# A perceiver layer with a mixture of experts: first loads in slices, last value tiles stored singly, middle stage and experts in one block, a value product ahead of local scores

## The chip, the cores and the metric

The kernel runs on one core of one Trainium2 chip, as one program. The metric is the time of one execution on the device, in microseconds (us). Three runs of the kernel before are given with their median, and beside them one profiled execution. TensorE is called PE, its weight loads PEld, VectorE DVE, ScalarE ACT, GpSimd POOL, and SP is the engine that issues most DMAs.

## The reference, cut to what matters

```python
x = x + xattn(layernorm(x), ctx, ctx, mask)     # 16 heads, 2 x 512 queries, 2 x 8192 keys
x = x + attn(layernorm(x))                      # local: window of 7 keys, latent 32x32 map on keys and values
x = x + ffn(layernorm(x))                       # shared MLP + 16 experts
def ffn(x):                                     # h = x as 1024 tokens of 512
    scores = sigmoid(h @ gate_w.T)
    topk_score, topk_ids = top_k(scores.T, 128) # each expert takes its 128 best tokens
    xin = h[topk_ids]
    eo = silu(xin @ gw.T + gb) * (xin @ up_w.T + up_b)      # 512 -> 2048
    eo = eo @ down_w.T + down_b                             # 2048 -> 512
    out = zeros.at[topk_ids].add(eo * topk_score)
    return out + (silu(x @ sh_gate.T) * (x @ sh_up.T)) @ sh_down.T
```

Everything is float32. Where the kernel multiplies in the fast format fp32r it splits both operands into a high and a low part and adds three products (high by high, high by low, low by high).

## The kernel before

The engines run programs of their own, written out by hand, and meet at semaphores. The program is cut into blocks; at the end of a block all five engines wait for one another.

**Context stage** (block at L176). The context (32 tiles of 512 tokens) is read tile by tile into CX; ACT makes the high part CH, DVE the low part CL, and PE makes keys (`keys`, L421: four banks, each 12 matmuls over the four quarters c of the contraction index) and values (`values`, L429). ACT and DVE evict, SP stores keys and values to memory (`stores`, L209 to L216). Ahead of the loop SP loads the key weights WK, the first context tile, the tokens X and then small constants (L218 on); ACT and DVE split WK and the tile, PE makes the first keys; DVE normalises X (`emit_layernorm`, L109 to L123), PE turns the normal tiles (L449) and makes the queries (L459). The last context tile is stored by `stores(NC_ALL - 1, 1)`: two key stores, then, when all four value tiles (128 tokens each, L286) are evicted, four value stores, one for each group of heads.

**Between** lies a block (L500) that is skipped unless a bound on the scores fails. The flag is read by every engine.

**Attention** (block at L666). Scores (L721), exponentials (L796, L799), value products (L734), sums on DVE (L832). PE starts it with seven scores of data loaded during the context stage.

**Middle stage** (block at L933). Output projection, local attention, shared MLP, routing. PSUM banks 0 to 3 are used in turn in the order of the list ORDER: `claim` waits until the bank's earlier result is evicted, `filled` and `evicted` are the waits for a result and for its eviction. Local attention runs in `slot(b, k)` steps: PE turns the weights of step k - 2 (L1062) and makes the scores of step k + 1 (L1051, into banks 4 and 5), which must wait until DVE has scaled the scores of step k out of those banks (L1463); DVE then takes the maximum (L1468), ACT the exponentials (L1300), DVE normalises (L1487, L1490) and copies the turned weights out (L1481). Products of the middle stage (`product`, L1028) stand between slots: q0.. queries, k1.. keys, v0.. values, vl0.. latent values (L1039). The end of the stage: down products dn4 to dn7 (L1117), each added to X by DVE (L1507) and stored by SP (L998); between them the routing result is turned, DVE makes the token numbers, and POOL gathers the first expert's rows (L1010). PE turns those rows (`rows0`, L1262) after dn7. DVE splits the bias tables and the first three weight tiles (`weights_lo`, L883) between its additions.

**Experts** (block at L1622). 192 weight tiles of 1 MB pass through a ring of six raw buffers (SP, L871), ACT makes the high part (L878), DVE the low part (L883), and PE makes gate and up products (L1663, bias L1652), turns the hidden rows (L1683) and makes the down products (L1699). POOL gathers the other experts' rows (L1631) and scatters the results (L1645).

## Time and profile before

| | us |
|---|---|
| median of 3 runs | 2913.43 (2911.68 to 2914.97) |
| profiled execution | 2915.47 |
| its span, first to last instruction | 2913.7 |
| PE busy | 2856.8 (98%) |
| DVE busy | 2153.7 (74%) |
| ACT busy | 1697.8 (58%) |
| POOL busy | 90.0 (3%) |

A line of 40 digits gives the busy tenths of each engine in 40 equal slices of some 73 us; 9 is 90% or more. PEclk is the granted clock of PE in tenths of full speed.

```profile
PE   7999999999899999999999999999999999999998
PEld 4888888888644444344444443445554588888887
DVE  5544444444498989898989898957466798888887
ACT  3112111211398989898989898925351377777775
PEclk9999999999999999999999999999999999999999
```

The chain of waits, followed back from the last instruction, by engine and by line:

```profile
PE 20%; POOL 0%; DVE 0%; issue 0%; ACT 0%
PE PS L1663 12%; PE PS L1699 6%; PE PS L1652 1%; PE PS L1683 1%; PE PS L1712 0%; POOL out L1645 0%; DVE YO L1790 0%; DVE HTL L1778 0%; ACT HTH L1740 0%
```

Slices 1 to 11 are the context stage, 12 to 26 attention, 27 to 32 the middle stage, the rest the experts.

### The profile page before, as it was taken

To read this page: it belongs to the slowest core of one execution; us is meant where nothing else is said; L and a number is where in the kernel's file an instruction comes from. 1 tells how busy PE (TensorE), PEld (TensorE's weight loads), DVE (VectorE), ACT (ScalarE), POOL (GpSimd) and SP (SyncE) were. 2 spreads that over 40 slices of the span, in tenths; PEclk is the share of its full clock that TensorE was granted. 3 is DMA by queue.
4 is the path that set the end of the run, shared out by engine and by line. 5 is a ranking of instruction groups with operands and counts; after the bars stand their busy time and mean duration, and the time that the engine had idled before them with its cause. 6 is when DMAs were issued, how large, how long until landed. Compare 5 with 4: busy or idle time off the path is not lost. (4 is left out here: it accounts for less than half of the span.)

```text
span 2913.7 us, 36671 instructions
## 1 busy us (share of the span) xinstructions
PE 2856.8 (98%) x14229; PEld 1752.3 (60%) x14229; DVE 2153.7 (74%) x1586; ACT 1697.8 (58%) x2128; POOL 90.0 (3%) x43
## 2 busy tenths in 40 slices
PE   7999999999899999999999999999999999999998
PEld 4888888888644444344444443445554588888887
DVE  5544444444498989898989898957466798888887
ACT  3112111211398989898989898925351377777775
POOL 0000000000000000000000000000000320000000
PEclk9999999999999999999999999999999999999999
DMA  5555555555555555555555555520103399999995
GB/s 207 181 186 188 192 182 187 188 193 182 171 131 128 128 124 125 127 132 124 128 122 131 128 128 125 124 71 24 64 13 129 143 391 345 346 346 349 347 348 201
DMA packets 228186, 515.46 MB, mean 177 GB/s; under 512 B 17986, under 2 KB 83906, under 8 KB 198460
## 3 DMA queue, kind: packets, MB, share of 16 engines
q1 hardware_dynamic: 224460, 505.15, 55.1%
q0 software_dynamic: 3584, 8.39, 1.2%
q8 instruction: 92, 1.51, 0.2%
q14 instruction: 50, 0.41, 0.0%
HBM read 400.03 MB, written 113.44 MB: 176 GB/s over the span
## 5 line engine op out<-in xcount | busy, mean ns | idle before, releaser
L832 DVE TENSOR_TENSOR AC<-AC,PR 128x2048 f32<-128x2048 f32 x440 | 969.6, 2281 | 0.0
L796 ACT ACTIVATE PR<-PS 128x1024 f32<-128x1024 f32 x866 | 831.7, 1034 | 78.9 <-PE PS L721 78.8
L721 PE MATMUL PS<-QS,KS 128*128 128x512 f32 x2048 | 607.9, 422 | 22.2 <-PEq L500 8.8
L721 PEld LDWEIGHTS PS<-QS,KS 128*128 128x128 f32 x2048 | 345.4, 188 | 388.3 <-ACT PR L796 260.1
L734 PE MATMUL PS<-PR,VC 128*32 128x512 f32 x4096 | 492.5, 598 | 1.1 <-ACT PR L796 1.1
L883 DVE TENSOR_TENSOR WL<-RAW,WH 128x2048 fp32r<-128x2048 f32 x192 | 436.2, 2286 | 60.8 <-ACT WH L878 60.8
L370 ACT ACTIVATE KH<-PS,bk_s 128x512 fp32r<-128x512 f32 x128 | 88.0, 688 | 561.0 <-PE PS L421 561.0
L878 ACT ACTIVATE WH<-RAW 128x2048 fp32r<-128x2048 f32 x192 | 361.8, 1913 | 1.3 <-PEq L933 1.1
L277 DVE SCALAR_TENSOR_TENSOR KL<-PS,bk_s,KH 128x512 fp32r<-128x512 f32 x128 | 95.7, 750 | 268.7 <-ACT KH L370 268.7
L734 PEld LDWEIGHTS PS<-PR,VC 128*32 128x32 f32 x4096 | 106.9, 109 | 247.0 <-issue 245.6
L421 PE MATMUL PS<-CH,WKH 128*128 128x512 f32 x512 | 203.2, 397 | 12.5 <-DVE CL L272 12.5
L421 PE MATMUL PS<-CL,WKH 128*128 128x512 f32 x512 | 203.3, 397 | 0.0
L429 PE MATMUL PS<-WVH,CH 128*128 128x512 f32 x512 | 203.1, 397 | 0.0
L421 PE MATMUL PS<-CH,WKL 128*128 128x512 f32 x512 | 203.0, 397 | 0.0
L429 PE MATMUL PS<-WVH,CL 128*128 128x512 f32 x512 | 202.6, 396 | 0.0
L429 PE MATMUL PS<-WVL,CH 128*128 128x512 f32 x512 | 202.5, 396 | 0.0
L1663 PE MATMUL PS<-WL,XEH 128*128 128x512 f32 x512 | 201.1, 393 | 0.0
L1663 PE MATMUL PS<-WH,XEL 128*128 128x512 f32 x512 | 200.6, 392 | 0.0
L1663 PE MATMUL PS<-WH,XEH 128*128 128x512 f32 x512 | 200.4, 391 | 0.0
L286 DVE TENSOR_TENSOR VS<-PS,bv_s 128x512 f32<-128x512 f32 x128 | 85.1, 685 | 113.0 <-PE PS L429 113.0
L799 ACT ACTIVATE PR<-PS 128x512 f32<-128x512 f32 x158 | 95.6, 605 | 58.5 <-PE PS L721 58.5
L1740 ACT ACTIVATE HTH<-PS 128x512 fp32r<-128x512 f32 x64 | 38.3, 599 | 150.7 <-PE PS L1683 150.7
(200 smaller groups left out, 3298.3 us busy)
## 6 DMA issues: line engine op xcount, KB each, us to landing
KS<-kh_d SPq DMA_DIRECT2D x256, 256.0 KB
RAW<-in_gw SPq DMA_DIRECT2D x64, 1024.0 KB, 5.6
RAW<-in_up_w SPq DMA_DIRECT2D x64, 1024.0 KB, 5.1
RAW<-in_down_w SPq DMA_DIRECT2D x64, 1024.0 KB, 5.1
AT<-in_ctx SPq DMA_DIRECT2D x32, 1024.0 KB, 5.7
kh_d<-KH SPq DMA_DIRECT2D x32, 1024.0 KB, 4.4
kl_d<-KL SPq DMA_DIRECT2D x32, 1024.0 KB, 6.5
v_d<-VS SPq DMA_DIRECT2D x128, 256.0 KB, 3.0
```

Of the source, the lines that this page charges most:

```text
L277: v.scalar_tensor_tensor(KL[s][:, g, :], PS[:, g, :], bk_s[:, g:g + 1], KH[s][:, g, :].bitcast(F32), ALU.add, ALU.subtract).then_inc(s_kl, 1)
L370: nc.scalar.activation(KH[s][:, g, :], PS[:, g, :], ACT.Identity, bias=bk_s[:, g:g + 1]).then_inc(s_kh, 1)
L421: mm = pe.matmul(PS[:, g, :], w[:, c, g * P:(g + 1) * P], a[s][:, c, :], start=(k == 0), stop=(k == len(terms) - 1))
L429: mm = pe.matmul(PS[:, G + t, :], a[s][:, c, t * P:(t + 1) * P], w[:, c, :], start=(k == 0), stop=(k == len(terms) - 1))
L721: mm = pe.matmul(PS[:, take(*BANK[m]), :], KS[N % 2][:, j, t * P:(t + 1) * P], QS[bg % 2][:, j, :], start=True, stop=True)
L734: m = pe.matmul(PS[j * DH:(j + 1) * DH, OUTB, :], VC[N % 2][:, t, j * DH:(j + 1) * DH], PR[tile % BUFS][:, j, :], start=q == 0, stop=q == ...
L796: nc.scalar.activation(PR[tile % BUFS][:, 2 * hp:2 * hp + 2], PS[:, first:first + 2, :], ACT.Exp, scale=SCALE).then_inc(s_exp, 1)
L799: nc.scalar.activation(PR[tile % BUFS][:, 2 * hp], PS[:, first, :], ACT.Exp, scale=SCALE)
L832: v.tensor_tensor(a[i % 2][:], a[i % 2][:], p[:], ALU.add).then_inc(s_acc, 1)
L878: nc.scalar.activation(WH[n % PAIRS][:], RAW[:, n % RAWS], ACT.Copy).then_inc(s_hi, 1)
L883: nc.vector.tensor_tensor(WL3[n % PAIRS][:], RAW[:, n % RAWS], WH[n % PAIRS][:].bitcast(F32), ALU.subtract).then_inc(s_lo, 1)
L1663: m = pe.matmul(PS[:, bank, :], x[e % 2][:, c, :], w[:, c, :], start=False, stop=i == len(terms) - 1)
```

## The change

- The first loads go by quarters of the contraction index: SP issues WK quarter 0, context quarter 0, WK quarter 1 and so on, eight loads of 256 KB, then X in four loads of two token tiles. ACT and DVE split each quarter as it comes. PE makes the first keys with the quarter as the outer loop and the four banks within. The layernorm statistics wait for their pair of tiles.
- The last context tile's values are stored tile by tile: each of the four stores holds 128 tokens of all groups and waits for its own eviction.
- The experts' programs stand in functions called at the end of the middle stage's block; the end of block between them is gone. In its place PE waits for the evictions of dn5, dn6 and dn7 ahead of the first expert product. `rows0` is made ahead of dn7, with its place in ORDER changed; DVE splits the rows' low part ahead of adding dn7. ACT splits the fifth weight tile only when dn7 is complete. POOL's further gathers start when the bias tables are ready; SP's seventh weight tile follows the store of dn7.
- In local attention v00 goes ahead of scores 0, v01 ahead of slot 0, v02 between slots 1 and 2, v03 between slots 2 and 3.

```diff
             v = nc.vector
             for i in range(TT):
+                if i % 2 == 0:
+                    chain.engine.wait_ge(s_x[i // 2], 16)
                 n = chain.mark(v.bn_stats(tmp[:, i, 0:6], src[:, i, :]))
...
-                sp.dma_start(WK[:].bitcast(F32), wk).then_inc(s_wk, 16)
-                sp.dma_start(CX[0], ctx_t[0]).then_inc(s_cx[0], 16)
-                sp.dma_start(X[:], x.rearrange("(i p) d -> p i d", p=P)).then_inc(s_x, 16)
+                for c in range(DC):
+                    sp.dma_start(WK[:, c].bitcast(F32), wk[:, c]).then_inc(s_wk[c], 16)
+                    sp.dma_start(CX[0][:, c], ctx_t[0][:, c]).then_inc(s_c0[c], 16)
+                for i in range(TT // 2):
+                    sp.dma_start(X[:, 2 * i:2 * i + 2], x[2 * i * P:(2 * i + 2) * P].rearrange("(i p) d -> p i d", p=P)).then_inc(s_x[i], 16)
...
-                stores(NC_ALL - 1, 1)
+                n, s = NC_ALL - 1, 1
+                sp.wait_ge(s_kh, n * G + G)
+                sp.dma_start(kh_d[:, n].rearrange("g p k -> p g k"), KH[s][:].bitcast(F32)).then_inc(s_kvst[s], 16)
+                sp.wait_ge(s_kl, n * G + 2 * G)
+                sp.dma_start(kl_d[:, n].rearrange("g p k -> p g k"), KL[s][:].bitcast(F32)).then_inc(s_kvst[s], 16)
+                for t in range(KT):
+                    sp.wait_ge(s_vs, n * KT + KT + t + 1)
+                    sp.dma_start(v_d[:, n, :, t, :].rearrange("g p d -> p g d"),
+                                 VS[s][:, t, :].rearrange("p (g d) -> p g d", g=G)).then_inc(s_kvst[s], 16)
...
-                dve.wait_ge(s_whi, 1)
-                v.tensor_tensor(WKL[:], WK[:].bitcast(F32), WKH[:].bitcast(F32), ALU.subtract).then_inc(s_wlo, 1)
-                split(0, 0)
-                dve.wait_ge(s_x, 16)
+                for c in range(DC):
+                    last = c == DC - 1
+                    if last:
+                        dve.wait_ge(s_whi, 1)
+                    else:
+                        dve.wait_ge(s_fhi, 2 * c + 1)
+                    v.tensor_tensor(WKL[:, c], WK[:, c].bitcast(F32), WKH[:, c].bitcast(F32), ALU.subtract
+                                    ).then_inc(s_wlo if last else s_flo, 1)
+                    if last:
+                        dve.wait_ge(s_chi, 1)
+                    else:
+                        dve.wait_ge(s_fhi, 2 * c + 2)
+                    v.tensor_tensor(CL[0][:, c], CX[0][:, c], CH[0][:, c].bitcast(F32), ALU.subtract
+                                    ).then_inc(s_clo if last else s_flo, 1)
                 emit_layernorm(chain, X, XN, tmp, s_xn, 1)
                 dve.wait_ge(s_small, 80)
                 key_lows(0, 0)
...
-                act.wait_ge(s_wk, 16)
-                nc.scalar.activation(WKH[:], WK[:].bitcast(F32), ACT.Copy).then_inc(s_whi, 1)
-                split(0, 0, 0)
+                for c in range(DC):
+                    last = c == DC - 1
+                    act.wait_ge(s_wk[c], 16)
+                    nc.scalar.activation(WKH[:, c], WK[:, c].bitcast(F32), ACT.Copy).then_inc(s_whi if last else s_fhi, 1)
+                    act.wait_ge(s_c0[c], 16)
+                    nc.scalar.activation(CH[0][:, c], CX[0][:, c], ACT.Copy).then_inc(s_chi if last else s_fhi, 1)
...
-                pe.wait_ge(s_wlo, 1)
-                keys(0, 0)
+                for c in range(DC):
+                    if c < DC - 1:
+                        pe.wait_ge(s_flo, 2 * c + 2)
+                    else:
+                        pe.wait_ge(s_wlo, 1)
+                        pe.wait_ge(s_clo, 3)
+                    for g in range(G):
+                        for k, (w, a) in enumerate(((WKH, CH), (WKH, CL), (WKL, CH))):
+                            mm = pe.matmul(PS[:, g, :], w[:, c, g * P:(g + 1) * P], a[0][:, c, :],
+                                           start=(c == 0 and k == 0), stop=(c == DC - 1 and k == 2))
+                        if c == DC - 1:
+                            mm.then_inc(s_kps, 1)
...
-                 + [f"{w}1{f}" for f in range(FS) for w in "gu"] + ["dn4", "dn5", "topk", "dn6", "dn7", "rows0"])
+                 + [f"{w}1{f}" for f in range(FS) for w in "gu"] + ["dn4", "dn5", "topk", "dn6", "rows0", "dn7"])
...
+        def experts_gpsimd(pool):
+            def gather(e, landed):
+                nc.gpsimd.indirect_dma_start(XG[e], None, h_d, bass.IndirectOffsetOnAxis(ap=token[:, e:e + 1], axis=0)
+                                             ).then_inc(landed, 16)
+
+            pool.wait_ge(s_bs, 5)
+            gather(1, s_g1)
+            for e in range(2, 7):
+                gather(e, s_ga)
+            pool.wait_ge(s_out, 16 * TT)
+            for e in range(7, E):
+                gather(e, s_gb)
+            for e in range(E):
...
+            def gate(S):
+                if S >= 2:
+                    pe.wait_ge(s_si, S - 1)
+                if S == 0:
+                    evicted(pe, "rows0")
+                elif S % FC == 0:
+                    pe.wait_ge(s_xl, S // FC)
+                rows_product("g", S, S % 2)
...
+            pe.wait_ge(s_bs, 5)
+            for name in ("dn5", "dn6", "dn7"):
+                evicted(pe, name)
+            gate(0)
+            up(0)
...
+            for n in range(EARLY, 4):
+                split(n)
+            filled(act, "dn7")
+            for n in range(4, PAIRS):
+                split(n)
+            silu(0)
...
+                pe.wait_ge(s_wv6, 16)
+                product("v00", WV6, XT2[0], 0)
                 pe.wait_ge(s_ke, G)
                 evicted(pe, "q03")
                 scores(0, 0)
-                pe.wait_ge(s_wv6, 16)
+                product("v01", WV6, XT2[0], 1)
                 slot(0, 0)
-                product("v00", WV6, XT2[0], 0)
                 slot(0, 1)
-                product("v01", WV6, XT2[0], 1)
+                product("v02", WV6, XT2[0], 2)
                 slot(0, 2)
-                product("v02", WV6, XT2[0], 2)
+                product("v03", WV6, XT2[0], 3)
                 slot(0, 3)
-                product("v03", WV6, XT2[0], 3)
                 slot(0, 4)
                 for i in range(4, TT):
                     evicted(pe, f"t2{i}")
...
                 down(6)
-                down(7)
                 pe.wait_ge(s_g0, 16)
                 bank = claim(pe, "rows0")
                 for c in range(DC):
                     m = pe.transpose(PS[:, bank, c * P:(c + 1) * P], XG0[:, c * P:(c + 1) * P], ident[:])
                 m.then_inc(s_full[bank], 1)
+                down(7)
+                experts_tensor(pe)
...
                     weights_lo(dve, i - 5)
+                    if i == TT - 1:
+                        bank = filled(dve, "rows0")
+                        dve.wait_ge(s_xh, 1)
+                        v.tensor_tensor(XEL[0][:], PS[:, bank, :].rearrange("p (c t) -> p c t", c=DC), XEH[0][:].bitcast(F32),
+                                        ALU.subtract).then_inc(s_free[bank], 1)
                     add_down(i)
-                bank = filled(dve, "rows0")
-                dve.wait_ge(s_xh, 1)
-                v.tensor_tensor(XEL[0][:], PS[:, bank, :].rearrange("p (c t) -> p c t", c=DC), XEH[0][:].bitcast(F32),
-                                ALU.subtract).then_inc(s_xl, 1)
...
-                pool.wait_ge(s_to, 2)
-                gather(1, s_g1)
```

## Rows read from the trace of the kernel before

**Rows 1.** Table of stages: stretch, length, busy us (instructions) per engine, granted clock, DMA share, GB/s.

```profile
2330.00:2890.00 560.00, 560.00 (x2611) 462.68 (x2610) 498.91 (x332) 401.88 (x319) 59.32 (x19) 1.00 0.95 348
```

**Rows 2.** Timeline, start: start us, duration, engine, line, operation, shapes, [idle before <- releaser].

```profile
2.12 2.39 SPq L221 DMA_DIRECT2D ident<-in_ident  x1
...
5.67 1.91 ACT L374 ACTIVATE WKH<-KL 128x2048 fp32r<-128x2048 f32 x1 [3.65 <-DMA KL<-in_wk]
...
8.16 1.91 ACT L366 ACTIVATE CH<-AT 128x2048 fp32r<-128x2048 f32 x1 [0.58 <-DMA AT<-in_ctx]
...
10.11 2.29 DVE L272 TENSOR_TENSOR CL<-AT,CH 128x2048 fp32r<-128x2048 f32 x1 [0.20 <-ACT CH L366]
...
12.50 0.77 PE L421 MATMUL PS<-CH,WKH 128*128 128x512 f32 x1 [12.50 <-DVE CL L272]
...
17.33 0.47 PE L421 MATMUL PS<-CH,WKL 128*128 128x512 f32 x1
```

**Rows 3.** Timeline, start, layernorm statistics, normal tiles, and PE's next work.

```profile
14.11 4.85 DVE L109 BATCH_NORM_STATS2 ln_tmp<-X 128x6 f32<-128x512 f32 x8 [1.71 <-DMA X<-in_x]
...
21.21 3.75 DVE L123 TENSOR_SCALAR XN<-X,ln_tmp 128x512 f32<-128x512 f32 x8
...
26.03 1.04 PE L449 MATMUL PS<-ident,XN 128*128 128x128 f32 x8
```

**Rows 4.** DMA issues of the first 60 us: count, KB each, median us to landing.

```profile
qh_d<-QH SPq DMA_DIRECT2D x6, 256.0 KB, 2.1
```

**Rows 5.** Timeline of DVE, SP and PE, context stage to attention.

```profile
773.53 0.69 DVE L286 TENSOR_TENSOR VS<-PS,bv_s 128x512 f32<-128x512 f32 x1 [1.86 <-PE PS L429]
...
774.25 2.64 SPq L216 DMA_DIRECT2D v_d<-VS  x4
...
782.21 3.32 PE L721 MATMUL PS<-QS,KS 128*128 128x512 f32 x7 [8.78 <-PEq L500]
```

**Rows 6.** Timeline of PE and DVE, first local scores.

```profile
1975.56 1.14 PE L1051 MATMUL PS<-RAW,AT 32*122 32x128 f32 x16 [0.87 <-ACT AT L1274]
...
1978.18 1.14 PE L1051 MATMUL PS<-RAW,AT 32*122 32x128 f32 x16 [1.49 <-DVE EX L1463]
...
1979.25 5.40 PE L1028 MATMUL PS<-XT,WV 128*128 128x512 f32 x8
...
2002.25 3.70 PE L1028 MATMUL PS<-XT,WK 128*128 128x512 f32 x8
...
2013.61 1.05 PE L1071 MATMUL PS<-EX,RAW 128*32 128x122 f32 x32 [1.09 <-DVE RAW L1455]
...
2003.95 1.22 DVE L1463 SCALAR_TENSOR_TENSOR EX<-PS,RAW 122x1024 f32<-122x1024 f32 x1
```

**Rows 7.** Groups by line: shapes, count | busy us, mean ns | idle before, releasers.

```profile
L1463 DVE SCALAR_TENSOR_TENSOR EX<-PS,RAW 122x1024 f32<-122x1024 f32 x20 | 24.4, 1218 | 17.9 <-PE PS L1051 17.8
...
L1300 ACT ACTIVATE EX<-EX,NX 122x128 f32<-122x128 f32 x160 | 61.9, 389 | 16.0 <-PE PS L1062 11.7 <-DVE NX L1468 4.0
```

**Rows 8.** Table of stages, columns as in group 1, two stretches of low clock.

```profile
1980.15:1983.50 3.35, 3.35 (x5) 1.35 (x4) 2.51 (x4) 2.42 (x14) 0.00 (x0) 0.50 0.00 0
...
2307.83:2311.20 3.37, 3.37 (x9) 2.61 (x10) 1.73 (x1) 3.37 (x2) 2.44 (x3) 0.50 0.77 275
```

**Rows 9.** Timeline of PE, DVE and POOL, middle stage to experts.

```profile
2292.08 2.72 POOL L1010 DMA_INDIRECT AT<-h_d,token  x1 [101.18 <-DVEq L1599]
...
2298.66 0.68 DVE L1507 TENSOR_TENSOR X<-X,PS 128x512 f32<-128x512 f32 x1
...
2305.20 0.60 PE L1262 MATMUL PS<-ident,AT 128*128 128x128 f32 x4
...
2305.40 0.69 DVE L1507 TENSOR_TENSOR X<-X,PS 128x512 f32<-128x512 f32 x1 [1.06 <-PE PS L1117]
...
2307.70 0.64 PE L1652 MATMUL PS<-BIAS,PICK 128*128 128x512 f32 x1 [1.90 <-PEq L933]
...
2309.47 4.49 DVE L883 TENSOR_TENSOR WL<-RAW,WH 128x2048 fp32r<-128x2048 f32 x2 [2.24 <-ACT WH L878]
```

More of the change, by code:

```diff
@@ L931, in program @@
         YO = [se(f"YO{i}", [CAP, D]) for i in range(2)]
+        s_g1, s_ga, s_gb = sem("second_gathered"), sem("tokens_gathered"), sem("last_tokens_gathered")
+        s_si, s_hid, s_t, s_hth, s_htl, s_xt, s_y, s_sc = (sem(n) for n in (
+            "expert_silu", "expert_hidden", "hidden_turned", "hidden_hi", "hidden_lo",
+            "expert_rows_turned", "expert_output", "expert_scattered"))
+        XG = [XG0] + [AT[:, i, :] for i in range(2, 8)] + [X[:, i, :] for i in range(TT)] + [WO[:, 3, :]]
@@ new lines, in experts_sync @@
+        def experts_sync(sp):
+            for n in range(RAWS, len(TILES)):
+                load_raw(sp, n)
+        def experts_gpsimd(pool):
[10 more added lines that the diff above has]
+            for e in range(E):
+                pool.wait_ge(s_y, e + 1)
+                if e:
+                    pool.wait_ge(s_sc, 16 * e)
+                nc.gpsimd.indirect_dma_start(out, bass.IndirectOffsetOnAxis(ap=token[:, e:e + 1], axis=0), YO[e % 2][:], None,
+                                             compute_op=ALU.add).then_inc(s_sc, 16)
+            pool.wait_ge(s_sc, 16 * E)
@@ new lines, in experts_scalar, with silu, hidden_hi, rows_hi @@
+        def experts_scalar(act):
+            def silu(S):
+                act.wait_ge(s_used, NTH["g", S] + 1)
+                if S >= 2:
+                    act.wait_ge(s_hid, S - 1)
+                nc.scalar.activation(GE[S % 2][:], PS[:, S % 2, :], ACT.Silu).then_inc(s_si, 1)
+            def hidden_hi(S):
+                act.wait_ge(s_t, S + 1)
+                if S >= 2:
+                    act.wait_ge(s_used, NTH["d", S - 2] + 1)
+                nc.scalar.activation(HTH[S % 2][:], PS[:, 4, :].rearrange("p (f t) -> p f t", f=FT), ACT.Copy).then_inc(s_hth, 1)
+            def rows_hi(e):
+                act.wait_ge(s_xt, e)
+                if e >= 2:
+                    act.wait_ge(s_used, NTH["u", (e - 1) * FC - 1] + 1)
+                nc.scalar.activation(XEH[e % 2][:], PS[:, 7, :].rearrange("p (c t) -> p c t", c=DC), ACT.Copy).then_inc(s_xh, 1)
+            def split(n):
+                if EARLY <= n < len(TILES):
+                    weights_hi(act, n)
+            for n in range(EARLY, 4):
[4 more added lines that the diff above has]
+            silu(0)
+            for S in range(STEPS):
+                if S % FC == 2 and S // FC + 1 < E:
+                    rows_hi(S // FC + 1)
+                split(3 * S + PAIRS)
+                hidden_hi(S)
+                split(3 * S + PAIRS + 1)
+                if S + 1 < STEPS:
+                    silu(S + 1)
+                split(3 * S + PAIRS + 2)
@@ L1011, in _ @@
                                              ).then_inc(s_g0, 16)
+                experts_gpsimd(pool)
             @block.tensor
```

279 lines of the change are left out of this document (107 added, 172 removed).

## The prediction

> **What bounds the kernel now.** I read the page's totals and its 40 slices first: TensorE (PE) is busy in nine tenths or more of nearly every slice, so only those places matter where PE stands still or runs at half clock. The chain of waits that ended last lies on PE all the way back to the first expert product, and the table of stages shows why: in 560 us of the expert stage PE is busy for 560.00 while VectorE (DVE) has 61 us to spare [rows 1]. What comes ahead of such a stage moves its end one for one. So I went through the timeline for PE's gaps. Four places are touched by the change: the first 12.5 us [rows 2], the passage from the context stage to attention [rows 5], the first local scores [rows 6 to 8] and the passage to the experts [rows 8, 9].
>
> **The first loads (sliced by contraction index).** Now WK (1 MB) is usable at 5.67 and the context tile (1 MB more) at 8.16; ScalarE (ACT) rounds each in 1.91, DVE subtracts each in 2.29, and PE starts at 12.50, after the second subtraction [rows 2]. One MB thus comes in 2.49 us, a quarter in 0.62. The first quarters of WK and context land at about 5.67 - 3 x 0.62 = 3.8 and 4.4; by the 256 KB stores of the queries, which land 2.1 us after issue [rows 4], it would be 0.7 + 2.1 = 2.8 and 3.3. Then one ACT operation on 128x512 (0.48, a quarter of 1.91, to 0.69, what DVE takes for 128x512 from PSUM [rows 5]) and one DVE operation (0.57 to 0.69): PE starts between 4.6 and 6.0. I take 5.8, since it comes from the loads themselves. That is 6.7 us earlier.
> Does PE then run through? Its first matmuls start 0.43 us apart until 17.33, the 37 steps from there to 26.03, where the next work begins, are 0.235 long [rows 2, 3]. Twelve matmuls of the first quarter at the slow spacing last 5.1 us, until 10.9; the last quarter lands at about 8.2 and is split by 9.5. No later quarter is waited for. If the slow start is as long as now (4.8 us), the product ends at 26.03 - 6.7 = 19.3.
> What is late next is the layernorm. X is usable at 14.11 as before (the same 4 MB lie ahead), now in four parts, so that statistics (4.85 for 8 tiles, 0.61 each) end at 14.1 + 1.2 = 15.3 instead of 18.96. From there to the first normal tile it is 21.21 - 18.96 = 2.25, so XN comes from 17.6 on, 0.47 per tile [rows 3]; PE asks for it at 19.3. Cover 1.2 us, and if it is gone PE waits by as much. The key eviction on ACT keeps its distance to the product's end, as all four banks still fill within the last quarter, 0.7 apart. SP (the issuing queue) has 9 more issues ahead of the small constants; at 2.12 / 3, some 0.5 each, that is 4 us, but those loads stand behind X's data now as well (the constants' first issue took 2.39, held up [rows 2]). **Term: -6.7**, ends -5 (everything 1 us late and a longer slow start) and -7.5.
>
> **The last value tiles.** DVE evicts the last one at 773.53, SP issues its four stores from 774.25 to 776.89, 0.66 each, and PE, idle since 773.4, starts at 782.21, after two ends of blocks [rows 5]. With a store per tile three are out before, and SP is done at 774.9. PE's first scores need none of the stores, only the block ends, and the last to reach the first of them is SP; the 5.3 us from its last issue to PE's start move with it. **Term: -2.0**; ends 0 (if those 5.3 hang on something else) and -2.6 (if the 1 MB of stores still in flight lengthens them now).
>
> **Local scores.** Before: PE ends the last query product at 1974.7, waits 0.87, scores, waits 1.49 for DVE, scores, and has the first value product at half clock: 5.40 where k10 takes 3.70 [rows 6, 8]. That is 0.87 + 1.49 + 1.7 = 4.1 us. After, v00 fills the first wait (8 half-products of 0.43 = 3.43) and v01 stands between scores 0 and 1. But then scores 2 follow scores 1 directly, and the same 1.49 returns there; and v03 no longer stands between slots 3 and 4, so turning weights 2 waits for its own softmax. Walked on with the rows' durations (scores 1.07 of PE, eight exponentials of 0.39 = 3.1 of ACT, DVE's scaling 1.2, its maximum, a pass of the same size, 1.2, its normalising, such a pass and a reciprocal, 1.4 [rows 6, 7]): scores 4 end at 1997.1, DVE has weights 2 at 1998.3, PE waits 1.3, and 0.2 more before scores 5. So 1.5 + 1.3 + 0.2 = 3.0 of waits against 4.1. Product k10 would start about 1.2 to 1.6 earlier than 2002.25. But DVE's fifth scaling comes at about 2003.7 instead of 2003.95, and the five latent values behind it end DVE-bound, so the next PE work (2013.61 now) comes only some 0.8 earlier. **Term: -0.8** if the clock stays full. If it falls again, 1.7 us of PE work is lost, partly beside DVE: +0.5. Without any fall before or after, the new order would itself cost 0.6.
>
> **Middle stage and experts in one block, first rows ahead of the last down product.** Now: last down product, its eviction by DVE at 2305.40, first rows turned at 2305.20, 1.90 idle, then experts at 2307.70 with granted clock 0.50 (1.2 of 2.4 GHz) from 2307.83 to 2311.20 [rows 8, 9], which loses 1.7 us. The change does not remove the wait: PE now waits for dn7's eviction. The walk: dn6 ends at 2298.2; the gather of the first rows is issued at 2292.08 and is 2.72 long, so it is there by about 2297; turning takes 0.5; dn7 takes dn5's bank, whose eviction ends at 2298.66 + 0.68 = 2299.3, so PE starts dn7 at 2299.5, 0.7 idle; 16 half-products of 0.43 end at 2306.4; DVE evicts until 2307.25; PE goes on at 2307.4. So the place moves by 0.3 only. But 1.05 idle stands where 1.90 was, with no turning between. In the rows the clock fell after 1.9 idle, and after 0.87 + 1.49 with scores between; a wait of 1.09 at 2013.61 [rows 6] left it full. I take it as full: **term: -0.3 - 1.7 = -2.0**; ends -0.3 and -2.3. Moved along: the weight loads from the seventh tile on stand behind dn7's store on SP and go out at about 2307.8, as before; six of the fifteen further gathers leave POOL's queue 11 us earlier, in a stretch with little traffic, which is a small relief. The third and fourth weight splits on DVE come 2 us earlier. All this is hidden by PE's 560 of 560 us.
>
> A rule speaks against those gathers. DVE's subtraction with two SBUF inputs took 4.49 for two while POOL gathered [rows 9], its usual time, and by this row the sum has no term for it. The Trainium skill (SBUF — State Buffer, Who interferes with whom) says that such a DVE operation and a GpSimd operation that reads SBUF exclude each other for the whole instruction. By that rule the eviction of dn5 could stand behind a gather.
>
> **The sum.** 6.7 + 2.0 + 0.8 + 2.0 = 11.5, against the profiled execution's 2915.47 (span 2913.7 and 1.8 around it): 2904.0. The median of the runs shown, 2913.43, is 2.0 lower; half-clock stretches that some executions lack may be part of it, and those I have taken off already. I allow 0.5: **2903.5**.
>
> **Rivals.**
> (a) The start gains half: slices land singly, 0.5 us or more late each, or X's parts come 3 us later and PE waits for XN. Against it: the first two MB come at a steady rate [rows 2]. The term is -3.5: 2907.
> (b) The clock falls at one of the two places: +1.7 at the experts or +1.3 at the scores, or both: 2905 to 2906.5. For it: waits of 1.5 and 1.3 between short matmuls.
> (c) POOL's gathers hold DVE: dn7 waits for one gather more, 2.7 us at most: 2906.2.
> (d) The stores don't do what the edit says, since the block ends wait for landing: term zero, 2905.5.
> (e) Slower than before: SP chokes on small issues. One issue took 2.39 [rows 2]. If all twelve of the first loads took 2.0 us or more, X would be in at 26.7 or later, XN 3.5 behind it plus 0.5, and PE would start turning at 31 instead of 26; that eats the other 4.8. At 2.39 each it is about +4.5: 2918. Against it: that issue stood behind 4 MB, while 3 issues before it took 1.4 in all.
>
> **How the numbers follow.** Forecast 0.52, (a) 0.13, (b) 0.20, (c) 0.06, (d) 0.05, (e) 0.04. A change below 0.2% (5.8 us) can hardly be told from none here; the border is 2907.6. Faster: forecast, (b), (c), (d) and half of (a): 0.89. Same 0.07, slower 0.04. The low end adds the far ends of the first two terms, 2901.5, and the distance to the median: 2900.3; the high end takes in (b), (c), (d) and most of (a): 2908.
>
> **What would show it.** PE's first matmul at 5 to 7 us, the rows at L449's place (the turning of XN) at about 19.3; SP's last store 0.7 us long and PE's idle time before attention 6.8 instead of 8.8; idle times of about 1.5 and 1.3 among the local scores; a wait of about 1.0 before the first expert product and granted clock 1.00 after it. Wrong would be: PE waiting for XN, a granted clock of 0.5 at the experts, or PE idle inside the expert stage.

## The result: 7.3 us faster, 0.25%

| | median, us | lowest to highest |
|---|---|---|
| before | 2913.22 | 2911.68 to 2915.90 |
| changed | 2905.94 | 2904.65 to 2910.62 |

The ratio is 0.9976 [0.9967, 0.9985]. The forecast was 2903.5 in a range of 2900.3 to 2908.0: faster, as forecast, the range held, and the point 2.4 us too low. The profiled execution of the changed kernel took 2906.36 (span 2904.6, PE's mean granted clock 0.997) against 2915.47 (2913.7, 0.997).

Since PE is never idle for long, the whole difference can be read from the starts of a few PE groups in the two profiles. The stages, in us, between these starts (the "last query products" are the group of three ahead of the local scores):

| stage, by PE's start | before | changed | gained |
|---|---|---|---|
| start to the turning of XN | 26.03 | 19.98 | 6.05 |
| to the first attention scores | 756.18 | 753.56 | 2.62 |
| to the last query products ahead of the local scores | 1182.01 | 1181.86 | 0.15 |
| to the first weighted sum (scores stage, below) | 49.39 | 49.80 | -0.41 |
| to the second expert bias (through the block passage) | 298.73 | 296.95 | 1.78 |
| to the end of the span | 601.36 | 602.45 | -1.09 |
| sum | 2913.7 | 2904.6 | 9.1 |

**First loads**, timeline of the changed kernel, where [rows 2] and [rows 3] stood (start, duration, what, idle time before and who ended it; the window cuts the last row, 0.49 us per tile):

```profile
4.32 0.63 ACT L399 ACTIVATE WKH<-KL 128x512 fp32r<-128x512 f32 x1 [2.30 <-DMA KL<-in_wk]
...
10.05 0.64 ACT L401 ACTIVATE CH<-AT 128x512 fp32r<-128x512 f32 x1 [0.74 <-DMA AT<-in_ctx]
...
6.39 0.80 PE L474 MATMUL PS<-CH,WKH 128*128 128x512 f32 x1 [6.39 <-DVE CL L323]
...
10.82 0.63 PE L474 MATMUL PS<-CL,WKH 128*128 128x512 f32 x1
11.25 0.49 PE L474 MATMUL PS<-CH,WKL 128*128 128x512 f32 x1
...
19.98 1.04 PE L485 MATMUL PS<-ident,XN 128*128 128x128 f32 x8
...
11.33 5.39 DVE L111 BATCH_NORM_STATS2 ln_tmp<-X 128x6 f32<-128x512 f32 x8
...
18.98 1.46 DVE L125 TENSOR_SCALAR XN<-X,ln_tmp 128x512 f32<-128x512 f32 x3
```

The first quarter of WK is usable at 4.32 and the last quarter of the context at 10.05; PE starts at 6.39 and does not wait until XN is turned. Its first matmuls come 0.43 apart (eleven steps, as before) and the others 0.23. XN's first tile is there 0.5 us before PE asks for it.

What the 0.43 is can be read from the kernel before, at the experts, inside the second stretch of [rows 8], where the granted clock is 0.50 (timeline of PE):

```profile
2308.13 0.63 PE L1663 MATMUL PS<-WH,XEH 128*128 128x512 f32 x1
2308.56 0.63 PE L1663 MATMUL PS<-WL,XEH 128*128 128x512 f32 x1
```

The same shape has the same 0.43 and 0.63 there. So the start of the kernel runs at half clock. The windows view gives 1.00 for it only because the trace's granted-clock record has no entry before 11.45 (before: 17.49), and time without an entry counts as full. In all fourteen profiles the first entry begins within 0.25 us of the last matmul that comes 0.43 behind its predecessor, after 6 to 13 such steps.

**Last value tiles**, timeline of the changed kernel, where [rows 5] stood (DVE's eviction, SP's issue, PE and SP behind the block ends):

```profile
767.49 0.69 DVE L299 TENSOR_TENSOR VS<-PS,bv_s 128x512 f32<-128x512 f32 x1 [1.86 <-PE PS L455]
...
768.21 0.37 SPq L275 DMA_DIRECT2D v_d<-VS  x1
773.40 0.37 SPq L717 DMA_DIRECT2D WO<-in_wo  x1
...
773.54 3.33 PE L757 MATMUL PS<-QS,KS 128*128 128x512 f32 x7 [6.15 <-PEq L536]
```

One store of 0.37 is left behind the last eviction, where four took 2.64. PE's idle time is 6.15 instead of 8.78, and SP goes on 4.8 us after its last issue (5.2 before).

**Local scores**, timeline of PE in the changed kernel, where [rows 6] stood:

```profile
1976.39 1.14 PE L1287 MATMUL PS<-RAW,AT 32*122 32x128 f32 x16 [1.33 <-DVE EX L1701]
1977.46 5.40 PE L1264 MATMUL PS<-XT,WV 128*128 128x512 f32 x8
...
1991.51 1.05 PE L1298 MATMUL PS<-ident,EX 122*128 122x122 f32 x8 [1.22 <-DVE EX L1728]
...
2005.20 1.05 PE L1307 MATMUL PS<-EX,RAW 128*32 128x122 f32 x32 [1.23 <-DVE RAW L1693]
```

Both waits that the walk found are there (1.33 and 1.22, forecast 1.5 and 1.3 + 0.2), and so is a half-clock stretch: v02, 5.40 where the others take 3.70.

**Passage to the experts**, timeline of PE and DVE in the changed kernel, where [rows 9] stood:

```profile
2290.99 7.13 PE L1353 MATMUL PS<-XT,HS 128*128 128x512 f32 x16 [0.46 <-DVE X L1745]
2299.11 0.47 PE L1001 MATMUL PS<-BIAS,PICK 128*128 128x512 f32 x1 [0.98 <-DVE X L1745]
...
2302.15 0.40 PE L1001 MATMUL PS<-BIAS,PICK 128*128 128x512 f32 x1
...
2298.16 0.69 DVE L1745 TENSOR_TENSOR X<-X,PS 128x512 f32<-128x512 f32 x1 [1.62 <-PE PS L1353]
2298.77 4.49 DVE L919 TENSOR_TENSOR WL<-RAW,WH 128x2048 fp32r<-128x2048 f32 x2
```

PE waits 0.98 for the eviction of the last down product and runs at full clock behind it (the second bias, 13 matmuls on, comes 3.04 later; 4.64 before). DVE's split takes 4.49 for two beside POOL's gathers, its usual time. The gathers, though, wait for the splits (timeline of DVE and POOL, the same kernel):

```profile
2293.65 2.29 DVE L919 TENSOR_TENSOR WL<-RAW,WH 128x2048 fp32r<-128x2048 f32 x1
...
2294.26 2.49 POOL L981 DMA_INDIRECT AT<-h_d,token  x1 [0.30 <-issue]
2297.06 0.95 POOL L981 DMA_INDIRECT AT<-h_d,token  x1 [0.30 <-issue]
```

The first of these gathers begins during a split, which ends at 2295.94, and ends 0.81 behind it; the second meets no split and takes 0.95.

**Inside the expert stage** PE is idle for 0.58, which the prediction named as a sign of being wrong. The windows view of the changed kernel (stretch, its length, busy time of PE, PE's weight loads, DVE, ACT and POOL, granted clock, share of the DMA engines' time, GB/s):

```profile
2310.00:2330.00 20.00, 20.00 (x96) 16.53 (x95) 15.71 (x11) 13.97 (x12) 8.96 (x5) 1.00 1.02 413
2330.00:2370.00 40.00, 39.42 (x184) 32.36 (x183) 36.07 (x25) 29.98 (x24) 3.41 (x1) 1.00 1.01 409
```

ScalarE's longest waits for loads from 2300 to 2400 (us in total, times, longest):

```profile
ACT WH L914 <- DMA RAW<-in_gw: 3.5, 3, 1.7
```

The chain of waits between 2300 and 2340 (start, duration, what):

```profile
2308.31 17.84 DMA RAW<-in_gw
...
2326.17 1.93 ACT WH L914
...
2328.11 2.29 DVE WL L919
2330.41 0.61 DVE HTL L1133
```

And the PE row that it ends in, from the timeline:

```profile
2331.15 0.47 PE L1050 MATMUL PS<-WH,HTH 128*128 128x512 f32 x1 [0.58 <-DVE HTL L1133]
```

A weight load needs 17.84 us while the DMA engines are full, ACT waits for it, DVE splits it, and only then does DVE come to HTL, for which PE waits. All expert bias matmuls of the changed kernel start as far apart as before, to 0.01 us, but for this one place, which adds 0.86; the other 0.2 lies behind the last of them. What else runs while that load, issued at 2308.31, is under way are POOL's last nine gathers: they go from 2303.3 to 2320.2 here, and from 2319.6 to 2340.0 before.

### The profile page after: what moved, and what is told of

It reads as the page before. It is cut to its first block and busy times, and to the rows that moved or that the text cites. A ratio compares the mean times of both kernels' runs of the same rounds, so it can differ in the third digit from the quotient of the medians.

```text
span 2904.6 us, 36696 instructions
## 1 busy us (share of the span) xinstructions
PE 2856.2 (98%) x14229; PEld 1751.3 (60%) x14229; DVE 2153.9 (74%) x1592; ACT 1699.4 (59%) x2134; POOL 88.9 (3%) x43
## 5 line engine op out<-in xcount | busy, mean ns | idle before, releaser
L447 PE MATMUL PS<-CL,WKH 128*128 128x512 f32 x496 | 196.0, 395 | 0.0
L447 PE MATMUL PS<-CH,WKL 128*128 128x512 f32 x496 | 195.9, 395 | 0.0
L447 PE MATMUL PS<-CH,WKH 128*128 128x512 f32 x496 | 195.8, 395 | 0.0
```

The source lines that it names most:

```text
L447: mm = pe.matmul(PS[:, g, :], w[:, c, g * P:(g + 1) * P], a[s][:, c, :], start=(k == 0), stop=(k == len(terms) - 1))
```

## The experiments

Each was timed beside the kernel before, in three groups in which its median was 2913.35 (a_alone, c_alone, scores_undone, late_gathers), 2914.28 (first_two_and_scores, after_again, late_gate_early, respread_late_gate_early) and 2913.81 (the others). So medians of different groups can be compared to some 1 us only, and the 95% intervals of the ratios are 1.8 to 2.7 parts in a thousand wide, 5 to 8 us. The stages of every profile, taken as in the table above, tell more. "Half clock" is what the granted clock shows in the scores stage and at the first expert product. Outside these two places every profile has half clock at the start, at the passage to attention (6.8 us, in two profiles 10.2) and at the very end; the stage from the first attention scores takes 1181.8 to 1182.0 in all.

| kernel | XN turned | to attention | scores stage | half clock in it | to 2nd bias | half clock at the experts | rest | median |
|---|---|---|---|---|---|---|---|---|
| before | 26.03 | 756.18 | 49.39 | 3.4 us | 298.73 | 3.4 us | 601.36 | 2913.22 |
| changed | 19.98 | 753.56 | 49.80 | 3.4 | 296.95 | none | 602.45 | 2905.94 |
| a_alone | 20.39 | 756.04 | 47.71 | none | 297.13 | none | 601.38 | 2908.14 |
| c_alone | 26.34 | 756.33 | 47.68 | none | 296.94 | none | 601.61 | 2914.06 |
| tile_stores_alone | 25.14 | 753.61 | 51.03 | 6.8 | 298.73 | 3.4 | 601.53 | 2911.57 |
| scores_undone | 20.02 | 753.63 | 49.38 | 3.4 | 296.98 | none | 601.79 | 2907.48 |
| first_two_and_scores | 19.86 | 753.57 | 48.08 | none | 297.15 | none | 601.47 | 2906.22 |
| after_again | 20.16 | 753.55 | 51.10 | 6.8 | 296.99 | none | 602.77 | 2906.61 |
| late_gathers | 19.85 | 753.53 | 49.71 | 3.4 | 296.96 | none | 601.42 | 2906.00 |
| late_gate_early | 19.98 | 753.56 | 51.10 | 6.8 | 295.73 | none | 601.47 | 2904.39 |
| old_scores_late_gate_early | 20.20 | 753.66 | 50.70 | 6.8 | 295.77 | none | 601.41 | 2904.43 |
| scores_respread_alone | 19.94 | 753.72 | 46.69 | none | 296.95 | none | 602.72 | 2903.63 |
| respread_gate_early | 20.00 | 753.58 | 46.69 | none | 295.75 | none | 602.87 | 2902.70 |
| respread_late_gate_early | 20.54 | 753.54 | 46.69 | none | 295.76 | none | 601.65 | 2901.48 |

### One part at a time

**The sliced first loads alone** (and nothing else of the diff):

```diff
-                sp.dma_start(WK[:].bitcast(F32), wk).then_inc(s_wk, 16)
-                sp.dma_start(CX[0], ctx_t[0]).then_inc(s_cx[0], 16)
+                for c in range(DC):
+                    sp.dma_start(WK[:, c].bitcast(F32), wk[:, c]).then_inc(s_wk[c], 16)
+                    sp.dma_start(CX[0][:, c], ctx_t[0][:, c]).then_inc(s_c0[c], 16)
...
```

> The kernel before with the first loads in slices alone. Theory: PE's queries start 6.05 us earlier, as in the changed kernel (31.56 to 25.51), and since PE is busy without a break behind it, all of it reaches the end: 6 us less, some 2907. Rival: a part is given back later, because attention or the middle stage takes its old length from something other than PE: then less than 5 us at the end although the queries start 6 us earlier.

Measured: 2908.14 against 2913.35, ratio 0.9983 [0.9974, 0.9992], 5.2 us, less than the 6 expected. XN is turned at 20.39, 5.6 earlier, and the stages behind give nothing back, so the rival did not happen. This part is the largest share of the gain. Its profile has another message: the two blocks are still there, and PE waits as long ahead of the experts as in [rows 9], but no half clock follows (timeline of PE, first the scores, then the experts):

```profile
1972.34 1.14 PE L1079 MATMUL PS<-RAW,AT 32*122 32x128 f32 x16 [1.49 <-DVE EX L1491]
1973.40 3.70 PE L1056 MATMUL PS<-XT,WV 128*128 128x512 f32 x8
...
2300.18 0.47 PE L1680 MATMUL PS<-BIAS,PICK 128*128 128x512 f32 x1 [1.90 <-PEq L961]
2300.49 0.40 PE L1691 MATMUL PS<-WH,XEH 128*128 128x512 f32 x1
```

So the same waits can be followed by half clock or by full clock. It is no property of the order alone.

The first stage has a spread of its own. With the old loads XN is turned at 26.34 after 13 slow steps, 26.03 after 11 and 25.14 after 7, some 0.2 us for each step. With the loads in slices the eleven profiles lie between 19.85 and 20.54, and in eight of them PE waits for XN, by 0.14 to 1.12 us, the longest in respread_late_gate_early (timeline of PE):

```profile
20.54 1.06 PE L485 MATMUL PS<-ident,XN 128*128 128x128 f32 x8 [1.12 <-DVE XN L125]
```

**The stores tile by tile alone:**

```diff
-                stores(NC_ALL - 1, 1)
+                for t in range(KT):
+                    sp.wait_ge(s_vs, n * KT + KT + t + 1)
+                    sp.dma_start(v_d[:, n, :, t, :].rearrange("g p d -> p g d"), ...
```

> The kernel before with the stores of the last value tiles tile by tile, and nothing else. Theory: the stage from the turning of XN to the first attention scores lasts 753.6 us instead of 756.2, TensorE is idle for 6.15 instead of 8.78 ahead of attention, and the median is 2.6 us below the kernel before. Rival (the gain seen in the changed kernel came with the earlier first loads): 756.2 us, 8.78 idle and no difference.

Measured: 2911.57 against 2913.81, ratio 0.9991 [0.9982, 1.0], 2.2 us, by itself at the edge of the noise; the stage is 753.61 and PE idle for 6.21, as expected. It is the stage that shows the mechanism, here and in every kernel of the table that has this part (753.5 to 753.7 against 756.0 to 756.3). The same profile has both half-clock stretches (PE, timeline):

```profile
1976.09 6.48 PE L1036 MATMUL PS<-XT,WV 128*128 128x512 f32 x8
...
2305.63 0.47 PE L1660 MATMUL PS<-BIAS,PICK 128*128 128x512 f32 x1 [1.90 <-PEq L941]
2305.94 0.57 PE L1671 MATMUL PS<-WH,XEH 128*128 128x512 f32 x1
```

**The one block alone:**

```diff
-                 ... ["dn4", "dn5", "topk", "dn6", "dn7", "rows0"])
+                 ... ["dn4", "dn5", "topk", "dn6", "rows0", "dn7"])
...
+                experts_tensor(pe)
```

> The kernel before with the middle stage and the experts in one block alone (first rows ahead of dn7, PE waiting for dn7's eviction). Theory: the first expert products come 1.8 us earlier (place 0.2, full clock 1.6), but the weight loads do not, and PE waits about 1.1 us for the eleventh or twelfth weight tile in the fourth step; 0.7 us less at the end. Rival: that wait was chance or comes from the other parts of the change; then 1.8 us less at the end and no wait of PE for a weight tile.

Measured: 2914.06 against 2913.35, ratio 1.0001 [0.9992, 1.001]. Nothing that can be told from no change, and the interval is too wide to tell 0.7 from 0. Its profile has full clock at the experts (296.94) and, other than the theory had it, no wait of PE in the expert stage (601.61), though ACT waits for loads there too, by 2.4 in all. The rival's "no wait" is right and its 1.8 less at the end did not come.

**The one block left out** of the changed kernel is the other way round:

```diff
+                down(7)
                 pe.wait_ge(s_g0, 16)
...
-                down(7)
-                experts_tensor(pe)
```

> The changed kernel without its third part: middle stage and experts are two blocks again, and the first rows are turned behind the last down product. Theory (the block is worth only what its place gives, since the half-clock stretch at the experts in the profile of before was an accident of that execution, and the expert stage gives it back): from the first weighted sum to the first expert matmul 294.1 us instead of 293.9, the expert stage from its second bias 601.4 instead of 602.45, median 2905.2 to 2906.2, no slower than the changed kernel's 2905.9. Rival (the prediction's term of 2.0 for this part is lost): 2907.5 or more, with granted clock 0.50 at the first expert product in its profile.

Measured: 2906.22, beside 2906.61 for the changed kernel itself in the same group; expert stage 601.47, as the theory had it. The stages of the two-block profiles say why: 297.13 and 297.15 with full clock and 298.73 (twice) with half clock, against 296.95 to 296.99 in one block. So the place itself is worth 0.17, and half clock at the experts, 1.6 us, occurred in two of four two-block profiles and in none of the ten one-block ones. Whether the one block keeps the clock full or these are draws like those of the scores, fourteen profiles do not settle. What is gained that way went into the expert stage, below.

### The local scores

**The changed order undone:**

```diff
-                product("v00", WV6, XT2[0], 0)
                 scores(0, 0)
-                product("v01", WV6, XT2[0], 1)
                 slot(0, 0)
+                product("v00", WV6, XT2[0], 0)
                 slot(0, 1)
+                product("v01", WV6, XT2[0], 1)
...
```

> The changed kernel with the old order of the first local scores. Theory: the new order costs 0.4 to 0.9 us, since it moves the waits (1.33 and 1.22 between slots) instead of removing them; this kernel is 0.4 to 0.9 us faster than the changed one, and its slow group of times (2910 against 2905) is rarer if the half-clock stretches of the new order make it. Rival: the new order gains 0.8 as predicted; this kernel is 0.8 slower.

Measured: 2907.48, ratio 0.9978 [0.9969, 0.9987]; its profiled execution was 0.9 shorter than the changed kernel's, its median 1.5 longer than the changed kernel's first and 0.9 longer than its second, both from other groups and within the noise. My expectation was a miss: at full clock the old order is 0.4 better (47.7 against 48.1), but both orders are open to half clock. In the old order the stage took 47.7, 47.7, 49.4, 49.4, 50.7 and 51.0.

**The changed kernel once more**, no edit:

> The changed kernel itself, beside the other three. Theory (a fall of the clock at a given wait is an accident of the execution, not of the order): times of 2904.5 to 2907 with a few about 2910, and if its profile has no 0.50 stretch among the local scores, that stage lasts 48.0 to 48.3 us from the last query product to the first weighted sum instead of 49.8; the expert stage from its second bias lies between 601.4 and 602.5. Rival (the new order makes the clock fall each time, by its 1.33 us wait): 0.50 behind the third scores again, 49.7 to 49.9 us.

Measured: 2906.61 (2904.62 to 2910.53). No half clock behind the third scores this time, but a longer one later, behind the second wait (timeline of PE):

```profile
1990.06 1.70 PE L1298 MATMUL PS<-ident,EX 122*128 122x122 f32 x8 [1.22 <-DVE EX L1728]
...
1993.69 5.40 PE L1264 MATMUL PS<-XT,WK 128*128 128x512 f32 x8
```

The windows view of this stretch (columns as above, granted clock 0.54):

```profile
1989.80:1996.00 6.20, 5.94 (x27) 4.26 (x28) 6.13 (x16) 5.02 (x25) 0.00 (x0) 0.54 0.20 83
```

The changed order thus takes 48.1, 49.7, 49.8, 51.1 or 51.1: one of its waits is followed by half clock in four of five profiles. The rival (the same place each time) is out. The theory's 48.0 to 48.3 was meant for a profile without half clock in this stage, which this one is not; first_two_and_scores, with the same order, shows it with 48.08. The expert stage, 602.77, is above the expected 602.5.

**A third order**, which puts a product or another score ahead of each softmax that is still under way:

```diff
+                scores(0, 0)
                 product("v00", WV6, XT2[0], 0)
-                scores(0, 0)
-                product("v01", WV6, XT2[0], 1)
                 slot(0, 0)
+                product("v01", WV6, XT2[0], 1)
                 slot(0, 1)
-                product("v02", WV6, XT2[0], 2)
                 slot(0, 2)
-                product("v03", WV6, XT2[0], 3)
+                product("v02", WV6, XT2[0], 2)
                 slot(0, 3)
+                product("v03", WV6, XT2[0], 3)
                 slot(0, 4)
```

> The changed kernel with the local scores in the third order (scores 0, v00, scores 1, v01, scores 2 and turn 0, scores 3 and turn 1, v02, scores 4 and turn 2, v03, scores 5 and turn 3) and nothing else. Theory (what the changed order costs is its two waits and the falls of the clock that they bring on): the stage from the last query product to the first weighted sum 46.7 us at full clock, against 48.1, 49.8 and 51.1 seen in the changed order; median 2.5 to 3.5 below the changed kernel, about 2903, and the times of the runs within 2 us of each other, none about 2910. Rival (the falls come from elsewhere and the tight times of the kernel before it in this study were luck): a median of 2904.5 or more, and single times about 2910.

Measured: 2903.63 (2903.20 to 2903.77), ratio 0.9965 [0.9952, 0.9979]: 2.3 to 3.0 below the changed kernel's two medians (of other groups), the stage 46.69 with full clock. The 46.7 of the expectation was known from "All three" below, which ran earlier. Seen in the kernel that also has the two edits below (timeline of PE):

```profile
1967.23 1.14 PE L1290 MATMUL PS<-RAW,AT 32*122 32x128 f32 x16 [0.87 <-ACT AT L1514]
...
1979.09 1.14 PE L1290 MATMUL PS<-RAW,AT 32*122 32x128 f32 x16 [0.34 <-DVE EX L1704]
1980.16 3.70 PE L1267 MATMUL PS<-XT,WV 128*128 128x512 f32 x8
...
2002.59 0.63 PE L1310 MATMUL PS<-EX,RAW 128*32 128x122 f32 x16 [1.09 <-DVE RAW L1696]
```

PE's two waits are 0.87 and 0.34, and the 1.09 that the order of before has as well. In the three kernels with this order no profile has half clock there, and the times of each (five of each) lie within 1.1 us, where the changed kernel's eleven spread over 6.0. That the five times near 2910 of the changed kernel (three in its own runs, two in after_again) came from half clock in this stage follows only indirectly, from their mean clock (0.995 to 0.996 against 0.997 to 0.998) and from their absence here; none of them has a profile, so it is not shown.

### The experts

**The last nine gathers later:**

```diff
-            for e in range(7, E):
-                gather(e, s_gb)
             for e in range(E):
                 pool.wait_ge(s_y, e + 1)
+                if e == 1:
+                    for i in range(7, E):
+                        gather(i, s_gb)
```

> The changed kernel with the nine gathers of experts 7 to 15 (2.4 MB) moved behind the second expert's output. Theory: the DMA engines are full from the first expert product to about 2369 because the weight ring refills while these gathers run, and PE's wait of 1.1 us in the fourth step is the price; without them the twelfth tile lands 5 us earlier, the wait is gone and the kernel is 1.1 us faster than the changed one. Rival: the wait comes from the order of ACT's and DVE's splits; then it stays.

Measured: 2906.00 (2904.28 to 2910.18), ratio 0.9975 [0.9966, 0.9984]. The stage is 601.42 instead of 602.45, and the profiled execution 1.2 shorter; the median is no lower. The load that took 17.84 lands 12.3 after its issue here. ScalarE waits for no load any more (its longest waits from 2300 to 2400):

```profile
ACT HTH L1094 <- PE PS L1035: 24.9, 10, 4.0
```

The 1.1 is thus shown in the stage. That the scores' half clock drowns it in the median is likely and not shown.

**PE's wait for the last down product moved** to the second up product, which is the first to use that bank, with the late gathers kept:

```diff
-            for name in ("dn5", "dn6", "dn7"):
+            for name in ("dn5", "dn6"):
                 evicted(pe, name)
...
+                if S == 0:
+                    evicted(pe, "dn7")
                 if S + 1 < STEPS:
                     up(S + 1)
```

> The changed kernel with its nine last row gathers behind the second expert, and TensorE's wait for the eviction of the last down product moved from the first expert product to the second up product, whose bank it is. Theory (the 0.98 us wait is on the path, and the expert stage holds it once the gathers are out of the way): first expert matmul 293.0 us behind the first weighted sum instead of 293.9, stage from the second bias 601.4, median 1.0 to 1.8 below the changed kernel's, 2904.1 to 2904.9. Rival (the transfers are what bounds the first experts): the stage from the second bias is longer by the same 1.0, 602.4, with ScalarE waiting for a weight load, and the median is that of the kernel with late gathers, 2906.0.

Measured: 2904.39 (2902.70 to 2907.27), ratio 0.9964 [0.9951, 0.9978]: 2.2 below the changed kernel beside it, where 1.0 to 1.8 was expected. To the second bias it is 295.73, 1.2 less than 296.95, and the stage behind keeps it (601.47). The same with the scores of before:

> Late gathers and the wait for the last down product moved, as in the 2901.5 us kernel, but the local scores in the order of before. Theory (0.87 and 1.49 us of waiting, 1.0 us more than in the third order, and a fall in about half of the executions): scores stage 47.7 us, or 49.4 with a fall, times in two groups about 2902.5 and 2904.2, median 2902.5 to 2904. Rival (the order of before never cost anything): the median of the 2901.5 us kernel within 0.4.

Measured: 2904.43 (2903.48 to 2905.38), ratio 0.9968 [0.9956, 0.998], 50.70 in the scores stage with 6.8 us at half clock. The two groups of times that I expected did not show; the median is 0.4 above the expected ones, and 3.0 above "All three" below, so the rival is out.

**All three**, third order, late gathers, moved wait:

> As the one before, and the local scores in a third order: scores 0, v00, scores 1, v01, scores 2 and turn 0, scores 3 and turn 1, v02, scores 4 and turn 2, v03, scores 5 and turn 3. Theory: TensorE waits 0.9, 0.6 and 1.0 us instead of 1.33 and 1.22, the clock stays full, and the stage from the last query product to the first weighted sum lasts 48.0 us (49.8 in the changed kernel, 47.7 in the old order at full clock); median 1.5 below the kernel before it in this list. Rival (a fall comes as often here): the stage is 49.4 to 49.8 us long and the medians are equal within 0.5.

Measured: 2901.48 (2900.79 to 2901.82), ratio 0.9954 [0.9941, 0.9968], 5.1 below the changed kernel beside it and the fastest of all. It is 2.9 below late_gate_early (1.5 expected), and the scores stage is 1.3 shorter than expected. And the same with the gathers early again:

> The 2901.5 us kernel with the nine last gathers back where the changed kernel has them, ahead of the first expert's output. Theory (gathers on a full DMA system hold back the weight loads of the first experts): the expert stage from its second bias 602.4 us instead of 601.5, ScalarE waiting for weight loads by 3 us or more in its first 60 us, median 0.6 to 1.0 above 2901.5. Rival (that cost is an accident of single executions): 601.5 to 601.7 and a median within 0.4 of 2901.5.

Measured: 2902.70 (2902.44 to 2902.95), ratio 0.9962 [0.9949, 0.9976], stage 602.87: 1.2 in both, where 0.6 to 1.0 was expected. With no half clock in the scores stage or at the experts the times of the two kernels do not overlap, so the cost of the early gathers shows in the medians too, though they come from two groups. Its place, by PE's timeline:

```profile
2327.34 0.47 PE L1050 MATMUL PS<-WH,HTH 128*128 128x512 f32 x1 [0.99 <-DVE HTL L1135]
```

## Why the prediction was near, and where it failed

- **First loads, -6.7: 6.05 in the profile, right mechanism, size 0.65 off.** The first quarter of WK was taken as there at 3.8, by dividing the time of the whole load; it came at 4.32, and a row for a single small load on an idle system was what I lacked. ScalarE took 0.63 for 128x512, within my bracket, and not a quarter of 1.91. PE started at 6.39, outside my 4.6 to 6.0. In this profile no later quarter and no XN was waited for, and SP did not choke (rival e): its quarter loads took 0.39 to 0.43 each to issue, 0.47 apart ("2.12 / 3, some 0.5" was a slip, 2.12 / 3 is 0.71). But rival (a) was nearer than it looks. The last quarter was usable at 10.05 and not at 8.2, DVE came to the statistics at 11.3 and ran all eight back to back until 16.7, not 15.3; of the cover of 1.2 in front of XN 0.5 was left, and eight of the eleven profiles with these loads have none. PE waiting for XN was a sign of being wrong, and there it shows, by 1.12 at most. That the slow start was 11 steps in both profiles compared is luck: over the fourteen it varies by 7 steps, some 1.4 us, and a shorter one does little for the new loads, since PE then comes to the unfinished XN (first_two_and_scores: 6 steps, and 0.65 of waiting).
- **Last value tiles, -2.0: 2.62**, my far end. I left 0.66 for the last store; it took 0.37, and SP's way from its last issue to the next block became 0.4 shorter. Rival d is excluded by the stage in tile_stores_alone.
- **Local scores, -0.8: +0.41, wrong in sign.** Waits and order were walked rightly, and "the new order would itself cost 0.6" was measured as 0.4 (48.08 against 47.7). The step that failed is "if the clock stays full". I priced the one fall of [rows 8] as belonging to the old waits and gave rival b 0.20; in the runs four of five executions in the changed order had half clock there, as four of six in the old.
- **One block, -2.0: 1.78 up to the second bias, 0.7 in the end.** Two steps failed. First, 1.6 of it was the half clock of one profiled execution; a_alone has the same 1.90 of waiting and full clock, so the place alone gives 0.17, and c_alone's median shows no gain. Of the distance between profile and median, 2.0, I allowed 0.5; since the term and the distance hold the same stretch, more of it belonged there. Second, "all this is hidden by PE's 560 of 560 us": a stage in which PE never stood still had no slack at its start in the transfers. The DMA engines are full from 2310 to 2370, and the last nine gathers, which the walk left out, now run 16 us earlier, among the weight loads that refill the ring. One late load reached PE through ScalarE and DVE: of the six kernels with one block and early gathers it cost 0.86 here, 1.28 twice, 1.18, 0.23 and in c_alone nothing; 0 with late gathers. The six gathers that the prediction did name, "a small relief", stay early in late_gathers (601.42 against 601.36): neither relief nor cost shows.
- **POOL's gathers against DVE (rival c)**: DVE was not held. Its splits took 2.27 to 2.34 each, with a gather under way or without, over all fourteen profiles, and dn7 waited 0.46 against my 0.7. It was POOL that waited, which the prediction did not ask: 128 of 210 gathers (the first expert's left out) began during a split, and these took 1.0 to 3.1 us and ended 0.81 to 0.88 behind it; the other 82 took 0.94 to 0.98, also beside evictions, and in seven cases with a split just begun or just ending. POOL is off the path, so this cost nothing. The rule of the Trainium skill (SBUF — State Buffer, Who interferes with whom) is that a DVE operation with two SBUF inputs and a GpSimd operation that reads SBUF exclude each other. The trace agrees for a gather that begins during a split; no split here is seen to wait for a gather.
- **The sum**: 11.5 forecast and 9.1 measured between the profiles; 9.9 forecast and 7.3 measured between the medians. The range held because it had room for rivals (b) to (d): (b) happened at the scores, and the loss in the expert stage was in none of them. Its low end does not add up either: 2904.0 - 0.8 - 0.6 is 2902.6, not 2901.5.

## What to carry to other kernels

Take a profiled execution's half-clock stretches as one draw: compare its time with the median of the runs first, and only count such a stretch as gain if several profiles have it or the waits around it go away. Where PE waits for several softmax steps, spread the independent products so that the waits shrink instead of moving; here 0.87 and 0.34 in place of 1.33 and 1.22 gave 1.4 us at full clock, and no half clock was seen in three profiles. And a stage with PE at 100% is not proof against an earlier start: look whether its transfers are full, and issue what is needed last behind what is needed first.

## What the runs showed of the hardware

- TensorE's granted clock fell to 0.50 (1.2 of 2.4 GHz) after a wait of 1.90 us in two profiles and stayed full after the same wait in two others; after waits of 0.87 and 1.49 it fell in four profiles of six, after 1.33 and 1.22 in four of five, after 0.87 and 0.34 in none of three. A stretch lasted 3.4 or 6.8 us in the granted-clock record and cost 1.6 to 1.7 or about 3.0 to 3.3 us.
- The kernel starts at half clock: the first 6 to 13 steps between matmuls are 0.43 us, as long as those recorded at 0.50, and the granted-clock record begins where they end. A view that says 1.00 there has no entry to go by. The number of steps differs between executions.
- A 1 MB weight load that takes 5.4 to 6.0 us from issue to landing in the median of the changed kernel's page took 17.84 us with the DMA engines at a share of 1.02 and 413 GB/s and POOL's gathers beside it, and 12.3 us in late_gathers, where the engines were as full (1.01) without the gathers.
- A gather of POOL (256 KB of rows) took 0.94 to 0.98 us of POOL; when it began during a DVE subtraction of two SBUF tiles it ended 0.81 to 0.88 us behind that subtraction, 1.0 to 3.1 us in all. The subtraction took 2.27 to 2.34 with a gather or without.
